# VectorE's long two-input instructions beside GpSimd's gathers and scatters, written as short ones: four graph layers on one core

## Time and profile before

| | |
|---|---|
| median of 3 runs | 6555.59 us (6553.88 to 6563.34) |
| the profiled execution: its span, first to last instruction | 8635.1 us |
| busy in it: PE, PE's weight loads | 47%, 31% |
| busy: DVE | 4326.1 us, 50%, 14882 instructions |
| busy: ACT | 2282.2 us, 26% |
| busy: POOL | 4305.3 us, 50%, 4026 instructions |
| DMA | 684.96 MB, 79 GB/s over the span |

### The profile page before, as it was taken

How to read it: one execution, slowest core, us unless ns; L and a number is a source line. 1 busy time by engine, 2 the same in 40 slices (tenths; PEclk the granted TensorE clock), 3 DMA queues, 4 the chain that set the end, 5 groups by cost and what they waited for, 6 DMA issues and landing times. The chain is left out here.

```text
span 8635.1 us, 76490 instructions
## 1 busy us (share of the span) xinstructions
PE 4016.2 (47%) x19708; PEld 2671.9 (31%) x19708; DVE 4326.1 (50%) x14882; ACT 2282.2 (26%) x5999; POOL 4305.3 (50%) x4026
## 2 busy tenths in 40 slices
PE   1111158312888825654563664342465476567000
PEld 0000034101555514443442443332344355233000
DVE  3010069301999944434432553565244698677553
ACT  0000000001777621110110333354111133799000
POOL 5777720575000046546555674774555100888577
PEclk8555589655999955555555555555666666798555
DMA  1111100000222222222222343343122144555222
GB/s 42 47 46 47 47 19 0 21 1 5 103 113 107 99 70 79 69 73 64 69 68 63 112 128 112 94 139 112 44 68 68 77 161 163 125 146 138 76 82 77
DMA packets 413612, 684.96 MB, mean 79 GB/s; under 512 B 283685, under 2 KB 290444, under 8 KB 407978
## 3 DMA queue, kind: packets, MB, share of 16 engines
q1 hardware_dynamic: 282410, 542.14, 17.7%
q0 software_dynamic: 130944, 140.05, 7.5%
HBM read 310.94 MB, written 373.78 MB: 79 GB/s over the span
## 5 line engine op out<-in xcount | busy, mean ns | idle before, releaser
L711 POOL DMA_INDIRECT G<-states,srcq x1568 | 1678.9, 1071 | 851.1 <-issue 479.5
L1133 DVE TENSOR_TENSOR_SCAN R<-same,R,G 128x28 f32<-128x28 f32 x4480 | 883.8, 265 | 622.1 <-issue 499.9
L1793 PE MATMUL PS<-ident,HH 128*128 128x128 f32 x2357 | 529.8, 376 | 1257.4 <-ACT AT L2063 373.2
L2063 ACT COPY AT<-PS 128x512 f32<-128x512 f32 (+1 forms) x494 | 283.7, 581 | 2467.3 <-remote 1375.1
L1793 PEld LDWEIGHTS PS<-ident,HH 128*128 128x128 f32 x2357 | 402.8, 205 | 1332.9 <-issue 409.9
L711 POOL DMA_INDIRECT EE<-node_info,srcq x392 | 394.4, 1006 | 545.0 <-DMA node_info<-XC 415.7
L1701 PE MATMUL PS<-R 128*128 128x392 f16 x784 | 283.0, 361 | 673.2 <-remote 375.7
L711 POOL DMA_INDIRECT G<-states,srci x392 | 406.7, 1038 | 321.0 <-ACT HH L2161 199.1
L1808 PEld LDWEIGHTS PS<-WD,AT 128*128 128x128 f32 x2358 | 505.8, 316 | 183.0 <-issue 182.7
L1808 PE MATMUL PS<-WD,AT 128*128 128x64 f32 x2358 | 560.6, 416 | 0.0
L824 POOL DMA_INDIRECT out_nodes<-O,dstq x392 | 430.9, 1099 | 188.2 <-issue 123.3
(11 more groups left out here) (412 smaller groups left out, 10157.6 us busy)
## 6 DMA issues: line engine op xcount, KB each, us to landing
states<-O SPq DMA_DIRECT2D x70, 896.0 KB, 3.6
HH<-states SPq DMA_DIRECT2D x56, 896.0 KB
total<-R SPq DMA_DIRECT2D x56, 896.0 KB
XB<-resid SPq DMA_DIRECT2D x42, 896.0 KB
states<-HH SPq DMA_DIRECT2D x28, 896.0 KB, 3.9
G<-states,srcq POOLq DMA_INDIRECT x1568
resid<-XB SPq DMA_DIRECT2D x28, 896.0 KB
xl_of_src<-O SPq DMA_DIRECT2D x14, 1792.0 KB
```

Source lines behind the costliest of these rows:

```text
L711: return pool.indirect_dma_start(to, None, table_, bass.IndirectOffsetOnAxis(ap=idx, axis=0), bounds_check=bound, oob_is_err=False).then_i ...
L1133: last = dve.tensor_tensor_scan(out=out_[:, order, f], data0=flags[:, order], data1=in_[:, order, f], initial=initial[:, f:f + 1], op0=ALU ...
L1793: last = pe.transpose(PS[:, 4 + k, q * P:(q + 1) * P], HH[:, b, (g * G4 + q) * D2:(g * G4 + q + 1) * D2], ident[:])
L2063: act.copy(AT[:, k, 0:n * P], PS[:, 4 + k, 0:n * P]).then_inc(s_copied, 1)
```

## The change

A helper `by_parts` writes one `tensor_tensor` over 28 columns as seven over 4 columns (256 elements in each partition). It takes the place of `tt` in `operands`, `new_states`, `gathered` (layer 3), `spread`, `node_add` (16 columns, four parts), `scores2`, `result` and `weighted2`. In `scores2` the feature-major product goes in eight parts of 8 features (224 elements), and so does the long scan; the leaky ReLU goes in seven parts. The parts have no wait between them; the wait or the semaphore increment stays with the last one. For one column (the patches between stages) nothing changes. Everything else, the order of the work, the buffers and the gathers, is as before.

```diff
+        FEATS_AT_ONCE = 8
...
+            def by_parts(out_, in0, in1, op, size=G4):
+
+                n = out_.shape[1]
+                for at in range(0, n, size):
+                    some = slice(at, min(at + size, n))
+                    last = tt(out_[:, some], in0[:, some], in1[:, some], op)
+                return last
...
                 if k < 3:
-                    return tt(left, r, per_row(inv_in, i, INV_FT, n), ALU.mult)
-                step(tt(left, r, per_row(rs_in, i, RSIN_FT, n), ALU.mult))
+                    return by_parts(left, r, per_row(inv_in, i, INV_FT, n), ALU.mult)
+                step(by_parts(left, r, per_row(rs_in, i, RSIN_FT, n), ALU.mult))
...
-                return tt(right, right, left, ALU.mult)
+                return by_parts(right, right, left, ALU.mult)
...
-                step(tt(XB[:, b, :], XB[:, b, :], O[:, b, 0:CD], ALU.add))
+                step(by_parts(cut(XB[:, b, :]), cut(XB[:, b, :]), cut(O[:, b, 0:CD]), ALU.add))
...
-                        step(tt(cut(G[:, b, :]), cut(G[:, b, :]), over(rs_src[:, bass.ds(i * C, C)], D), ALU.mult))
+                        step(by_parts(cut(G[:, b, :]), cut(G[:, b, :]), over(rs_src[:, bass.ds(i * C, C)], D), ALU.mult))
...
-                step(tt(cut(XB[:, b, :]), cut(XB[:, b, :]), over(tail[:, at], D), ALU.mult))
+                step(by_parts(cut(XB[:, b, :]), cut(XB[:, b, :]), over(tail[:, at], D), ALU.mult))
...
-                tt(RN[k % 3], RN[k % 3], XN[k % 7], ALU.add).then_inc(s_nadd, 1)
+                by_parts(cut(RN[k % 3]), cut(RN[k % 3]), cut(XN[k % 7]), ALU.add).then_inc(s_nadd, 1)
...
-                step(tt(turned, XB[:, b, :].rearrange("p (t f) -> p f t", f=D), tail[:, at].unsqueeze(1).broadcast_to([P, D, C]), ALU.mult))
+                step(by_parts(turned, XB[:, b, :].rearrange("p (t f) -> p f t", f=D), tail[:, at].unsqueeze(1).broadcast_to([P, D, C]), ALU.mult, FEATS_AT_ONCE))
...
-                dve.tensor_tensor_scan(out=one[:, ::-1], data0=flags[:, ::-1], data1=XC[:, ::-1], initial=0.0,
-                                       op0=ALU.mult, op1=ALU.add).then_inc(s_scan2, 1)
+                for f in range(0, CD, FEATS_AT_ONCE * C):
+                    some = slice(f, f + FEATS_AT_ONCE * C)
+                    last = dve.tensor_tensor_scan(out=one[:, some][:, ::-1], data0=flags[:, some][:, ::-1], data1=XC[:, some][:, ::-1], initial=0.0,
+                                                  op0=ALU.mult, op1=ALU.add)
+                last.then_inc(s_scan2, 1)
...
-                step(tt(cut(two), cut(NEAR[i % 4]), one.rearrange("p (f t) -> p t f", t=C), ALU.add))
-                step(dve.scalar_tensor_tensor(out=two, in0=two, scalar=0.2, in1=two, op0=ALU.mult, op1=ALU.max))
+                step(by_parts(cut(two), cut(NEAR[i % 4]), one.rearrange("p (f t) -> p t f", t=C), ALU.add))
+                for g in range(GROUPS):
+                    some = two[:, g * G4 * D:(g + 1) * G4 * D]
+                    last = dve.scalar_tensor_tensor(out=some, in0=some, scalar=0.2, in1=some, op0=ALU.mult, op1=ALU.max)
+                step(last)
...
-                step(tt(cut(two), cut(two), attb2[:].unsqueeze(1).broadcast_to([P, C, D]), ALU.mult))
+                step(by_parts(cut(two), cut(two), attb2[:].unsqueeze(1).broadcast_to([P, C, D]), ALU.mult))
...
-                step(tt(cut(o), cut(r), inverse, ALU.mult))
-                step(tt(cut(o), cut(o), bias2b[:].unsqueeze(1).broadcast_to([P, n, D]), ALU.add))
-                return tt(o, o, xb, ALU.add)
+                step(by_parts(cut(o), cut(r), inverse, ALU.mult))
+                step(by_parts(cut(o), cut(o), bias2b[:].unsqueeze(1).broadcast_to([P, n, D]), ALU.add))
+                return by_parts(cut(o), cut(o), cut(xb), ALU.add)
...
-                step(tt(cut(G[:, b, :]), cut(G[:, b, :]), over(Eb[:, 0, at], D), ALU.mult))
+                step(by_parts(cut(G[:, b, :]), cut(G[:, b, :]), over(Eb[:, 0, at], D), ALU.mult))
```

## The result

| | us |
|---|---|
| kernel before, median of 4 runs | 6554.74 (6538.55 to 6563.34) |
| changed kernel, median of 4 runs | 6402.72 (6388.11 to 6410.11) |
| ratio | 0.977, 95% interval 0.975 to 0.9789 |
| forecast | 6365 (6260 to 6510) |

152 us faster, inside the range, 38 us short of the forecast's 190. The profiled execution of the changed kernel took 6388.11 us, with a span of 6386.4: it lies with its own runs.

The account below looks back on a forecast made before the run. The prediction took POOL's gathers, stalled by two-input DVE instructions, as the bound, with ACT next in att2. Gains of 29 + 22.5 + 32 + 9 + 31 + 75 - 8 = 190 us gave 6365 us, range 6260 to 6510.

Parts of the forecast that it names:

- The mechanism: Gathers on POOL wait for a two-SBUF-input DVE instruction to end, finishing 0.87 us after it; 325 us of stall in all.
- The layers at POOL's floor: Layers 0 to 3 lie near POOL's floor in the runs, so a gather's stall is time; about 84 us gained.
- Recording causes these pauses: The profiled execution's 2079.5 us above the median put down to recording; 1871 us of it found in pauses and waits.
- Rival A: Layers and att1 lie above POOL's floor in the runs too: 61 us gained, 6495 us; chance 0.20.
- What remains of the stall: After cutting, a gather waits 0.17 us on average for a part: 0.29 us left for each split instruction.
- att1 and sum2: First attention and last sum: POOL's stall shrinks, gaining 9 us in att1 and 31 in sum2.
- att2: Second attention: ACT bounds it once gathers are freed, 596 us for 671, so 75 us gained and not POOL's 118.
- the rest of the waits: In att2, ACT's 67.8 us of waits for DVE's statistics fall to a rest of 10 to 17 us.
- Rival C: A gather isn't let in between parts, so each stall lasts the whole run of parts: 129 us slower, 6685 us; chance 0.07.
- B: More stalls in the runs than recorded (layers 2 and 3 about 100 us, ACT freer in att2): 6300 us; chance 0.12.
- D: The stalls stay, by another cause that comes with these instructions: no gain, 6565 us; chance 0.05.
- Its signs: Changed profile: L711's longest gathers below 1500 ns, POOL busy 250 us less, att2 about 596 us, ACT over 93%, sum2 about 566.

Follow-up runs that it names:

- e9: The changed kernel plus one unused two-input product of 1792 elements, whole, per chunk in layers 0 and 1: 6436.32 us.
- e4: The changed kernel with everything that is cut in two parts (896 elements) instead of seven or eight: 6438.26 us.
- e11: The changed kernel plus one whole one-input reduction of 1792 elements per chunk in layers 0 and 1: 6408.48 us.
- e2: The changed kernel with the parts undone in att1, att2 and sum2, so only the layers are cut: 6467.74 us.
- e1: The kernel before, without any edit, profiled a second time: 6548.86 us, span 6547.2 us.
- the earlier trace: First profile of the kernel before, which the prediction read; an execution held up by something no trace shows: span 8633 us for runs of 6555.
- e7: The changed kernel with every second gather of att2 left out, so scores of those columns use old rows: 6355.19 us (one run).
- e3: The changed kernel with the parts undone in the layers, att1 and sum2, so only att2 is cut: 6532.26 us.
- e8: The changed kernel with parts of 1 column or 2 features (64 or 56 elements): 6901.17 us.
- e10: The changed kernel plus one unused two-input product per chunk in layers 0 and 1, in seven parts of 256 elements: 6408.04 us.
- e5: The changed kernel with the edge stage's two additions per chunk (L1195, L1200) in seven parts too: 6374.37 us.

## Why the prediction was right, and where it was wrong

- **The mechanism**, right. The gather is held from about 0.13 us after its start to the end of the two-input instruction (e9's longest, 2.64 us), let in between parts of 896 elements and, but for nine gathers, of 256 (e4, after), and indifferent to a reduction with one input (e11). The Trainium skill (SBUF — State Buffer, Who interferes with whom) infers that `tensor_tensor` leaves descriptor generation alone. e9 against e11 speaks against that inference: here a `tensor_tensor` costs a gather 1.2 us and a reduction of the same length next to nothing.
- **The layers at POOL's floor**, right: 84 forecast, 83 by e2's median, 74 between the two profiles, and e1 shows them back to back before the change. Its reason was wrong, so that it came out is in part luck. "Recording causes these pauses" does not hold: neither e1 nor the changed kernel's profile has them. Rival A, built on that execution, falls with it. The sizes inside come from that execution too: layers 0 and 1 lost 9.7 and 10.3 us of POOL's busy time (14.5 each forecast), layer 2 17.2 (22.5), layer 3 36.1 (32), 73 together.
- **What remains of the stall**, 0.29 us for each split instruction forecast: layer 0 has (394.41 - 392 x 0.997) / 14 = 0.26, but layer 2 only 0.11 and layer 3 0.12.
- **att1 and sum2**, a little low: 9 + 31 forecast, 50 by the difference of the medians, 56 with sum1 in the two profiles.
- **att2**, the step that failed. "Those 67.8 are DVE sitting behind late gathers, so they go too": they went to 54.8 only, and the stage to 641 us and not 596. The mis-sized term is the rest of the waits, 54.8 for 10 to 17. Two things are in it. 32.5 us are the stage's start, as before the change (32.8 of the 67.8, among them the 23.7 of the earlier trace rows). The longest, 22.1 now, follows DVE's wait for the first chunk's 28 gathers, which take 28 x 1.3 = 36 us without any stall. The other 22.3 are behind the loads of R, for which DVE waits 67.9 us and in the earlier trace rows 17.2. With half the gathers both shrink and the stage is 601 (e7). The rest of ACT's sum was right: 563.7 + 15.4 + 5 = 584, and the stage less these waits of ACT is 584 to 588 us in the changed kernel and e3 to e7. Both could be read, the start as the longest wait of the earlier trace rows, the loads as the smaller releaser beside a larger one in the earlier trace rows. The 38 to 45 us of this term are as much as the whole shortfall of 38.
- **Rival C**, given 0.07: not so at 256 elements but for 9 gathers of 354, and so for 230 of 373 at 64 (e8). The argument against it (a gather was let in at L1596's end although L1629 had started) used instructions of 1.2 and 2.0 us and said nothing of short ones.
- **Rivals A, B and D** (6495, 6300, 6565): the median of 6403 is nearest to the forecast itself. A's 98 instructions are 126 by the prediction's own list (42 + 42 + 28 + 14), which would put A at 6508. B's stronger stalls are not there: 63 us in layers 2 and 3 of e1, for the 79 of the earlier trace rows and B's 100, and ACT in att2 no freer than recorded. D's other cause is ruled out by e9 against e10 and e11.
- **Not in the forecast**: the edge stage. It left L1195 and L1200 out because the change does, but they stall POOL by 38 us there, and some 20 us of time could be had (e5).
- **Its signs.** POOL's busy time (394 us in layer 0, 421 in att2, 246 less than e1 over the seven stages for 250) and DVE's 16572 instructions came nearly as forecast. Missed were the longest gathers of att2 (2446 ns, not below 1500), its length, ACT's share of it (88%, not over 93) and sum2, 553 us for 566.

## What to carry to other kernels

If gathers run back to back, look for vector instructions with two SBUF inputs beside them. One of 2 us costs the gathers 0.5 us (L1305) to 1.5 us (L1191) on average in e1, by when a gather meets it; a reduction of the same length costs nothing. Cut them, but not fine: parts of 256 elements here brought 152 us, of 896 elements 113, of 128 nothing, and of 64 a loss of 355. Cut only in stages where the gathering engine sets the end. Before summing a gain, take out the waits that no faster gather removes, such as a stage's first, and look at the second releaser of each other wait, since the freed engine's traffic can make it late.

## What the runs showed that was not expected

- A run of short parts can hold a gather as one long instruction does, across two operations as well: 5.40 us with 128 elements in a part and 7.40 with 64, both ending 0.87 to 0.88 us after the last part. The parts start 0.135 us apart with 64 elements, 0.202 with 128 and 0.336 with 256, each about 0.08 us before the one before has ended, so it is not a gap that makes the difference; what does stays open. Short scans, 0.176 us apart in runs of 64, don't do it: of 890 gathers that meet them in the changed kernel none takes over 1.11 us.
- It matters how long the run has gone on when the gather comes. With 64 elements, 15 of the 150 gathers that come in a run's first microsecond are held and 215 of the 223 that come later; with 128, 13 of 164 and 165 of 262; with 256, 0 of 173 and 9 of 181. No kernel here tests whether shorter runs would keep the gathers free.
- Among parts of 256 elements, those of L1638, which read one input turned, take 623 ns and hold gathers more often (4 of 12); one shows in the changed kernel's timeline, DVE and POOL:

```profile
5197.42 3.29 DVE L1143 TENSOR_TENSOR HH<-G,HH 128x256 f32<-128x256 f32 x6
5200.74 2.44 DVE L1641 SCALAR_TENSOR_TENSOR HH<-HH 128x256 f32<-128x256 f32 x7
```

```profile
5199.22 2.37 POOL L712 DMA_INDIRECT G<-states_xl,dsti  x1 [0.30 <-issue]
```

- It ends at 5201.59, 0.88 us after the last part of L1638 (5200.71) and in the middle of L1641's parts.
